# Moving the rotation of the queries from VectorE to GpSimd, with the halves placed by DMA

## The reference

```python
# 1: linear attention, 32 heads of 8
qkv = relu(x @ Wqkv.T);  vk = [v, 1]^T k per head;  y = (vk q)[:8] / (vk q)[8];  y @ Wp.T + bp
# 2: cross attention, 16 heads of 16, keys and values from ctx
q = rope2d((x @ Wq.T).astype(float16), pos);  k = rope2d((ctx @ Wk.T).astype(float16), pos)
softmax(q k^T / 4) v @ Wo.T + bo
# 3: low-rank FFN
gelu(x @ U1 @ V1 + b1) @ U2 @ V2 + b2
```

## Time and profile before

| | |
|---|---|
| Time, median of 3 runs (lowest to highest) | 702.24 us (699.44 to 704.75) |
| The profiled execution | 699.2 us, of which the span is 697.4 us |
| Busy in the span | TensorE 566.8 us (81%), VectorE 460.2 (66%), ScalarE 344.3 (49%), GpSimd 283.2 (41%) |
| Mean granted TensorE clock | 0.905 of full speed |
| The chain that ended last, by engine | TensorE 55%, VectorE 20%, issue 12%, GpSimd 4%, ScalarE 4%, SP's queue 3%, DMA 2% |

### The profile page before, as it was taken

The page is one execution under the profiler, slowest core; times in us unless marked ns, Lnnn a source line. Parts: engine busy times, 40 slices in busy tenths (PEclk is TensorE's granted clock), DMA queues, the critical chain, the costliest instruction groups (busy, mean ns, idle before and its releaser), DMA issues.

```text
span 697.4 us, 11782 instructions
## 1 busy us (share of the span) xinstructions
PE 566.8 (81%) x4224; PEld 384.8 (55%) x4224; DVE 460.2 (66%) x954; ACT 344.3 (49%) x503; POOL 283.2 (41%) x305
## 2 busy tenths in 40 slices
PE   2664778979797979798888979797978677899994
PEld 1554555747474747475656656565655444455552
DVE  5226578787878777787878787878777852234344
ACT  5220235646364646364545455554645545655551
POOL 4454304336353536262626262626161422232344
PEclk9987889999898989898989898989897978999998
DMA  7632101010202010101010101111000000113232
GB/s 273 143 99 59 40 0 55 2 53 3 67 4 66 6 64 7 62 9 62 12 58 24 45 24 47 31 39 48 7 24 1 24 16 16 46 49 117 90 120 91
DMA packets 24650, 34.94 MB, mean 50 GB/s; under 512 B 5080, under 2 KB 10840, under 8 KB 24600
## 3 DMA queue, kind: packets, MB, share of 16 engines
q1 hardware_dynamic: 23880, 33.85, 15.2%
q10 hardware_dynamic: 720, 0.43, 0.2%
HBM read 23.51 MB, written 8.65 MB: 46 GB/s over the span
## 4 chain that ended last, share of the span: by engine, by line
PE 55%; DVE 20%; issue 12%; POOL 4%; ACT 4%; SPq 3%; DMA 2%; POOLq 0%; DVEq 0%; ACTq 0%
PE FR L1039 19%; PE BK L1205 8%; PE BK L1039 6%; PE SC L1163 5%; DVE q_grp L849 5%; PE FR L1121 5%; DVE nmax L900 4%; PE SC L1190 4%; DVE q_grp L848 4%; PE FR L1097 2%; PE FR L1250 2%; DVE lin_tm L812 2%; POOL rs L546 2%; POOL c_fm L551 2%; PE BK L1222 1%
## 5 line engine op out<-in xcount | busy, mean ns | idle before, releaser
L658 ACT ACTIVATE probs<-SC 128x1024 f32<-128x1024 f32 x128 | 130.7, 1021 | 91.1 <-PE SC L1190 91.0
L900 DVE TENSOR_REDUCE nmax<-SC 128x4 f32<-128x1024 f32 x128 | 156.1, 1220 | 26.9 <-PE SC L1163 25.8
L1205 PE MATMUL BK<-probs,v_aug 128*32 128x256 f32 x1024 | 81.6, 443 | 0.6 <-ACT probs L658 0.6
L482 POOL TENSOR_TENSOR rs<-ve,minus_half 128x2 f32<-128x2 f32 x16 | 11.2, 701 | 164.0 <-DVE nm L942 164.0
L1163 PE MATMUL SC<-k_blk,q_grp 48*128 48x512 f16 x256 | 54.4, 422 | 15.7 <-DVE nmax L900 15.4
L1121 PE MATMUL FR<-ident,lin_tm 128*128 128x128 f32 x64 | 16.8, 414 | 61.3 <-DVE lin_tm L812 61.3
L1190 PE MATMUL SC<-q_grp,k_blk 64*128 64x256 f16 x512 | 54.0, 292 | 3.7 <-ACT q_grp L616 1.8
L463 POOL TENSOR_TENSOR att_fm_l<-att_raw,att_fm_h 128x512 fp32r<-128x512 f32 x16 | 20.5, 1278 | 80.4 <-ACT att_raw L634 80.4
L728 ACT ACTIVATE probs<-SC,b_ff 128x512 f32<-128x512 f32 x64 | 39.8, 686 | 22.4 <-PE SC L1356 21.7
L1039 PE MATMUL FR<-w_qkv_h,xs_fm_h 128*128 128x512 f32 x64 | 29.8, 466 | 23.0 <-POOL xs_fm_l L427 13.8
L1205 PEld LDWEIGHTS BK<-probs,v_aug 128*32 128x32 f32 x1024 | 29.2, 121 | 33.0 <-issue 23.6
(11 more groups left out here) (170 smaller groups left out, 1660.7 us busy)
## 6 DMA issues: line engine op xcount, KB each, us to landing
x_fm<-in_x_fm SPq DMA_DIRECT2D x16, 256.0 KB, 3.0
c_fm<-in_c_fm SPq DMA_DIRECT2D x16, 256.0 KB, 3.6
x_tm<-in_x_tm SPq DMA_DIRECT2D x16, 256.0 KB, 2.7
x_kept<-x2b SPq DMA_DIRECT2D x16, 256.0 KB, 2.2
x_tm<-x_kept SPq DMA_DIRECT2D x16, 256.0 KB, 2.7
out<-c_fm SPq DMA_DIRECT2D x16, 256.0 KB, 2.0
k_blk<-k_rope SPq DMA_DIRECT2D x128, 16.0 KB, 1.8
cos_t<-rope_tables SPq DMA_DIRECT2D x1, 896.0 KB
```

Source lines behind the costliest of these rows:

```text
L658: act.activation(probs[:, j % 4], SB[:], ACT.Exp, scale=SCALE).then_inc(s_exp, 1)
L900: dve.tensor_reduce(nmax[:, t, :, 2 * q:2 * q + 2], SA[:].rearrange("p (s f) t -> p s f t", s=2), AX.X, ALU.max, negate=True).then_inc(s_m ...
L1205: mm = pe.matmul(BK[q // 2][HP * k:HP * (k + 1), (q % 2) * T:(q % 2 + 1) * T], v_aug[b % NB][:, t, HC * q + k], probs[:, j % 4, k], start= ...
```

## The change

- **Queries on GpSimd.** VectorE keeps only the swap of halves. GpSimd's new `rope_q` makes the products in `k_cos` and `k_sin` (shared with the keys) and their sum, over all 128 partitions, in a new tile `q_rope`. It stands behind `rope_k` in GpSimd's step, ahead of `keep_x2`.
- **Placing.** SP's new `place_q` moves the four blocks of 32 partitions of `q_rope` into `q_grp`, behind `place_k`. `scores1` waits for these transfers.
- **First norm.** `stats1` also writes minus the mean (`nm1`), and GpSimd multiplies it by the power it has just made; `norm1_shift` goes.
- **Filling.** The keys of batch 0 are rotated and placed in step -2 and not in -3; those of batch 1 are made, rotated and placed in step -1. In the filling steps `residual_bias` stands ahead of the rotations.
- **Store of x2.** `keep` no longer waits for its own store; two semaphores alternate, and the waits stand where the buffer is used again.

```diff
 def key_batch(b):
-    return b + 3 if b < -1 else b + 2 if b >= 0 else -1
+    return b + 2 if b >= 0 else {FIRST: 0, -1: 1}.get(b, -1)
 ...
+def place_q(n):                                   # SP
+    sp.wait_ge(s_q_rope, n + 1)
+    wait(sp, s_s2_mm, NQ * (n - 2))
+    grp = q_grp[n % NB][:].rearrange("p (c e) t -> p e c t", e=2)
+    for e in range(2):
+        for s in range(2):
+            src, dst = PR * (e + 2 * s), TR * s
+            sp.dma_start(grp[dst:dst + PR, e], q_rope[src:src + PR]).then_inc(s_q_placed[n % NB], 16)
 ...
 def keep(q):
     sp.wait_ge(s_x2b, q + 1)
-    sp.dma_start(a["x2"][q], x2b[:, q % 2]).then_inc(s_x2_out, 16)
-    sp.wait_ge(s_x2_out, 16 * (q + 1))
+    sp.dma_start(a["x2"][q], x2b[:, q % 2]).then_inc(s_x2_out[q % 2], 16)
 ...
-    if on(key_batch(b)):                          # SP's step
+    if b == -2:
+        place_k(0)
+    if b >= -1 and on(key_batch(b)):
         place_k(key_batch(b))
+    if on(b + 2):
+        place_q(b + 2)
 ...
+def rope_q(n):                                    # GpSimd
+    cos, sin = (t[:, n * T:(n + 1) * T].unsqueeze(1).broadcast_to([P, CC, T]) for t in (cos_t, sin_t))
+    pool.wait_ge(s_q2_ev, n + 1)
+    pool.wait_ge(s_k_rope, n + 1)
+    pool.tensor_tensor(k_cos[:], q16[:], cos, ALU.mult).then_inc(s_q_part, 1)
+    pool.wait_ge(s_q_rot, n + 1)
+    pool.tensor_tensor(k_sin[:], rot[:], sin, ALU.mult).then_inc(s_q_part, 1)
+    if n >= 1:
+        pool.wait_ge(s_q_placed[(n - 1) % NB], 16 * N_Q_DMA * ((n - 1) // NB + 1))
+    pool.wait_ge(s_q_part, 2 * n + 2)
+    pool.tensor_tensor(q_rope[:], k_cos[:], k_sin[:], ALU.add).then_inc(s_q_rope, 1)
 ...
-    pool.wait_ge(s_ve1, n + 1)                    # rstd1
+    pool.wait_ge(s_ve1, 2 * n + 2)
     pool.tensor_tensor(rs1[:], ve1[:], minus_half[:], ALU.pow).then_inc(s_rs1, 1)
+    pool.wait_ge(s_rs1, n + 1)
+    pool.tensor_tensor(mr1[:], nm1[:], rs1[:], ALU.mult).then_inc(s_mr1, 1)
 ...
+    if b < 0:                                     # GpSimd's step
+        residual_bias(m)
+    if b == -2:
+        rope_k(0)
+    if b >= -1 and on(key_batch(b)):
         rope_k(key_batch(b))
+    if on(n):
+        rope_q(n)
     if on(q):
         keep_x2(q)
     if on(n):
         residual2(n)
-    if on(m):
+    if b >= 0 and on(m):
         residual_bias(m)
 ...
     turn_halves(rot, q16, s_q_rot)                # VectorE, rope_q
-    dve.tensor_tensor(q_cos[:], q16[:], cos, ALU.mult).then_inc(s_q_part, 1)
-    dve.wait_ge(s_q_rot, n + 1)
-    dve.tensor_tensor(q_sin[:], rot[:], sin, ALU.mult).then_inc(s_q_part, 1)
-def rope_q_sum(n):
 ...
-    for s in range(2):
-        src, dst = TR * s + PR, TR * s
-        dve.tensor_tensor(grp[dst:dst + PR, 0], q_cos[dst:dst + PR], q_sin[dst:dst + PR], ALU.add)
-        ins = dve.tensor_tensor(grp[dst:dst + PR, 1], q_cos[src:src + PR], q_sin[src:src + PR], ALU.add)
 ...
+    dve.tensor_scalar(nm1[:], mv1[:, :, 0], -1.0, None, ALU.mult).then_inc(s_ve1, 1)    # stats1
-def norm1_shift(n):
 ...
-    wait(pe, s_v2_ev, m if m < 3 else m - 1)      # q1
+    wait(pe, s_v2_ev, m if m < 2 else m - 1)
 ...
-    pe.wait_ge(s_q_rope, n + 1)                   # scores1, first chunk
+    pe.wait_ge(s_q_placed[n % NB], 16 * N_Q_DMA * (n // NB + 1))
```

More of the change, by code:

```diff
@@ L143, in build @@
         mr1 = sb("mr1", [P, TT])
+        nm1 = sb("nm1", [P, TT])
         nm2 = sb("nm2", [P, TT])
@@ L151, in build @@
         rot, k_rot = sb("rot", [P, CC, T], F16), sb("k_rot", [P, CC, T], F16)
-        q_cos, k_cos = sb("q_cos", [P, CC, T], F16), sb("k_cos", [P, CC, T], F16)
-        q_sin, k_sin = sb("q_sin", [P, CC, T], F16), sb("k_sin", [P, CC, T], F16)
+        k_cos = sb("k_cos", [P, CC, T], F16)
+        k_sin = sb("k_sin", [P, CC, T], F16)
         k_rope = sb("k_rope", [P, CC, T], F16)
+        q_rope = sb("q_rope", [P, CC, T], F16)
         q_grp = [sb(f"q_grp{i}", [P, HC, T], F16) for i in range(NB)]
@@ L211, in build @@
         s_k_const = sem("s_k_const")
-        s_x2_out = sem("s_x2_out")
+        s_q_placed = [sem(f"s_q_placed{i}") for i in range(NB)]
+        s_x2_out = [sem(f"s_x2_out{i}") for i in range(2)]
         s_x2_in = [sem(f"s_x2_in{i}") for i in range(2)]
@@ L263, in build @@
         N_W_REST = 8
-        N_K_DMA = 8
+        N_K_DMA, N_Q_DMA = 8, 4
         FIRST = -3
@@ L407, in _ @@
             for h in range(2):
+                sp.wait_ge(s_x2_out[h], 16)
                 fetch(0, h)
@@ L410, in _ @@
             keep(LAST)
+            for h in range(2):
+                sp.wait_ge(s_x2_out[h], 16 * (B // 2))
             with sp.Fori(0, NFB - 1) as i:
@@ L450, in rope_k @@
                 pool.wait_ge(s_k2_ev, n + 1)
+                wait(pool, s_q_rope, n)
                 pool.tensor_tensor(k_cos[:], k16[:], cos, ALU.mult).then_inc(s_k_part, 1)
@@ L491, in keep_x2 @@
                 pool.wait_ge(s_x2, 2 * q + 2)
-                wait(pool, s_x2_out, 16 * (q - 1))
+                wait(pool, s_x2_out[q % 2], 16 * (q // 2))
                 pool.tensor_tensor(x2b[:, q % 2], x2_tm[:],
@@ L505, in step @@
                     att_lo(p)
-                if on(key_batch(b)):
+                if b < 0:
[3 more added lines that the diff above has]
+                if b >= -1 and on(key_batch(b)):
                     rope_k(key_batch(b))
+                if on(n):
+                    rope_q(n)
                 if on(q):
@@ L830, in rope_q @@
                 turn_halves(rot, q16, s_q_rot)
[L831 to L836, removed]
-                dve.tensor_tensor(q_cos[:], q16[:], cos, ALU.mult).then_inc(s_q_part, 1)
-                dve.wait_ge(s_q_rot, n + 1)
-                dve.tensor_tensor(q_sin[:], rot[:], sin, ALU.mult).then_inc(s_q_part, 1)
-            def rope_q_sum(n):
-                wait(dve, s_s2_mm, NQ * (n - 2))
-                dve.wait_ge(s_q_part, 2 * n + 2)
-                grp = q_grp[n % NB][:].rearrange("p (c e) t -> p e c t", e=2)
-                for s in range(2):
-                    src, dst = TR * s + PR, TR * s
-                    dve.tensor_tensor(grp[dst:dst + PR, 0], q_cos[dst:dst + PR], q_sin[dst:dst + PR], ALU.add)
-                    ins = dve.tensor_tensor(grp[dst:dst + PR, 1], q_cos[src:src + PR], q_sin[src:src + PR], ALU.add)
-                ins.then_inc(s_q_rope, 1)
             def lint(n):
@@ L877, in stats1 @@
                 dve.tensor_scalar(ve1[:], mv1[:, :, 1], LN_EPS, None, ALU.add).then_inc(s_ve1, 1)
-            def norm1_shift(n):
-                dve.wait_ge(s_rs1, n + 1)
-                dve.scalar_tensor_tensor(mr1[:], mv1[:, :, 0], -1.0, rs1[:], ALU.mult, ALU.mult).then_inc(s_mr1, 1)
+                dve.tensor_scalar(nm1[:], mv1[:, :, 0], -1.0, None, ALU.mult).then_inc(s_ve1, 1)
             def ev_x1(n):
@@ L962, in step @@
                     row_max(n1, 2)
-                if on(n):
-                    norm1_shift(n)
                 if on(p):
@@ L987, in step @@
                     add2(p)
-                if on(n):
-                    rope_q_sum(n)
                 if on(m):
@@ L1156, in scores1 @@
                     pe.wait_ge(s_k_const, 16 * 2 * NB)
+                    pe.wait_ge(s_q_zeros, NB)
                 if c == 0:
                     pe.wait_ge(s_k_placed[n % NB], 16 * N_K_DMA * (n // NB + 1))
-                    pe.wait_ge(s_q_rope, n + 1)
+                    pe.wait_ge(s_q_placed[n % NB], 16 * N_Q_DMA * (n // NB + 1))
                 wait(pe, s_max, NQ * n + c)
```

## The result

| | before | after |
|---|---|---|
| Median of the runs compared (4 each) | 703.5 us | 627.12 us (624.73 to 628.47) |
| The profiled execution, its span | 699.2, 697.4 us | 624.73, 622.9 us |
| Ratio after / before | | 0.8919, 95% interval 0.887 to 0.8969 |
| Mean granted TensorE clock | 0.905 | 0.963 |

What follows compares the result with a forecast made beforehand. VectorE's four sums ahead of the divide, with the TensorE clock lost behind them, were taken as the bound. Ten steps save 55.6 us, steps 1, 2 and 13 9.6, filling and step 0 7.8: 73.0 off 699.2, 626 us, range 610 to 656.

Steps and rivals of the forecast that it cites:

- The wait and the clock: Ahead of the divide: removing VectorE's four sums saves 3.95 us, TensorE's clock staying full 2.7, less 0.6; 28.0 us a step.
- The placing path as the limit: Step's end: queries through GpSimd, SP and DMA land just after TensorE arrives, setting the step at 28.5 us.
- Work counted as nothing: Norm's product on GpSimd, 0 to 0.70 us, and keep's dropped wait on SP: both counted as no change in time.
- Steps 1 and 2: Two early steps, 32.06 and 33.54 us before, also to take 28.5: 3.6 and 5.0 us saved.
- Step 13: A step without divide, 25.81 us before: 1.0 us saved, bounds 2 lost and 3 saved.
- The filling: Before step 0: first scores at 64.2 to 64.8 instead of 67.5, 3.0 us saved; step -1 saves 2.4 us.
- The clock's loss: Rival, chance 0.12: gaps at the step's end keep TensorE's clock low, a step of 30.7 us, 652 us in all.
- the late placing: Rival, chance 0.14: dearer issues or slow landing of the queries add 2 to 4 us a step, 650 to 674 us.
- GpSimd stretches VectorE's work: Rival, chance 0.04: GpSimd and VectorE hinder each other, rope_q takes twice its 3.6 us, 644 us in all.

Runs made afterwards that it cites:

- Experiment 5: The changed kernel with GpSimd's rotation of the keys ahead of the low part of the attention output from step 0 on; 616.43 us.
- experiment 3: The changed kernel with twelve spare statistics instructions on VectorE ahead of the divide in steps 0 to 12, about 4.0 us; 694.65 us.
- experiment 2: The changed kernel with six spare statistics instructions on VectorE ahead of the divide in steps 0 to 12, about 2.0 us; 649.87 us.
- experiment 9: The changed kernel with the norm's product back on VectorE and SP again waiting for the store of x2; 624.8 us.
- experiment 4: The changed kernel with four more transfers per batch into a spare tile, between the four that place the queries; 682.48 us.
- Experiment 10: The changed kernel with keys rotated first and x of batch 2 loaded early (604.8 us), plus add2 moved behind row maximum 6 on VectorE; 607.84 us.
- experiment 8: The changed kernel with the queries' two products and one full-width sum back on VectorE, the placing by four transfers kept; 633.56 us.

## Why the prediction was right, step by step

The forecast was 626 us. The sum was made against the profiled execution, and that came out at 624.73; the median came out at 627.12.

- **The wait and the clock.** Put at 3.95 + 2.7 us less 0.6 for row maximum 6, a floor of 28.0 us a step. Experiment 5 has it bare at 28.0; experiment 3 shows wait and clock coming back together. Of the 2.7 us that the clock cost, the projection's part was taken too large: its twelve products take 1.61 us at full clock, not the 1.42 of the output projection with which they were compared, so 0.82 us and not 1.01 came back there. The clock's part was the least certain, argued from one step of the earlier trace rows; at the 2.1 us of gap of experiment 2 it fell in five of eleven steps.
- **The placing path as the limit.** Put at 28.5, measured 28.58, and right as a mechanism for eight of the ten steps. The other two were set by the shift and `add1` on VectorE, a path that the prediction did not have; that they came out at nearly the same length is luck. The parts: issues of the queries 2.6, measured 2.50; landing 1.8 from the issue, 1.9 at the median; from the last issue's end to the scores 1.2 to 1.8, measured 1.36; GpSimd's three 3.6, measured 3.6 (302.14 to 305.72 in the timeline). place_k's 8 issues were taken at 5.65 and took 5.98.
- **Work counted as nothing.** The norm's product and keep's wait: experiment 9 confirms it. The product itself took 0.20 us on GpSimd, against bounds of 0 and 0.70.
- **Steps 1 and 2.** 3.6 and 5.0 predicted, 4.0 and 5.9 measured. They came out at 28.07 and 27.65 us, below the 28.5 that I took over from the later steps. Step 2 ends by the third path; beyond that it was not followed why.
- **Step 13.** 1.0 gained was predicted, 0.9 lost: the step starts and ends with the clock low in part, and the path through eight and four issues is bare, 3.6 us of waiting. It lay within the bounds given (2 lost).
- **Step 14** was left out of the sum and gained 2.3 us: the same work stands there, but the clock is back sooner, as in the turns of L1235, 0.79 and 0.44 us in the chain against 1.04 and 0.85 before. Steps 13 and 14 together came out at 1.4 gained, against 1.0 summed.
- **The filling.** 5.4 up to step 0, measured 6.2. The load that lands late was put at 47.9 and came at 48.4; the first scores at 64.2 to 64.8, came at 64.26.
- **The rivals.** The clock's loss and the late placing did not happen here, but both are real further on: experiments 2 and 4. That GpSimd stretches VectorE's work happened, though not as the rival had it: GpSimd's own rotation kept its 3.6 us, but the shift's second operation takes 808 ns on average after, against 181 before. In most steps the wait for the placing hides it; at the end of step 2 and of the first two like steps it stands on the chain.

```profile
L926 DVE TENSOR_SCALAR shift<-nmax_c 128x32 f16<-128x32 f32 x16 | 12.9, 808 | 0.6
```

In experiment 10 such operations stood on the path in the step shown. The Trainium skill (GPSIMD Engine Reference, Key points) names VectorE's instructions in a 2-port mode beside those with two SBUF inputs. This one reads a single SBUF tensor; that it slows down fits the page, while no run here shows its mode. The Trainium skill's advice to keep elementwise work on VectorE (GPSIMD Engine Reference, Engine selection) is borne out only where nothing disturbs VectorE, 0.42 us against GpSimd's 1.15 for a half-precision operation of 128x512: experiment 8 followed it, and there the second product and the sum took 1.37 and 1.38 us on VectorE in nine of ten steps, longer than on GpSimd.

## What to carry to other kernels

Cost an edit by the gap that it closes on the engine that sets the step, and count the clock with it: here 4 us of idle TensorE cost another 2.7 us. When work moves off that path, compute the next path's end as carefully as the saving; here the sum of the placing's issues came within 0.1 us of the mean step. Look also at what stays on the engine that was relieved: operations of 0.18 us that were off the path took up to 1.2 us beside the other engine's work and, in some steps, came onto it. If an operation is split into pieces only to move data between partitions, one full-width operation and a few small transfers can be the shorter way, provided that the transfers have several us before they are needed; that it beats moving the pieces to another place in the order was not tried here.

## What was not expected of the hardware

The clock is not a function of the gap alone: with one and the same gap of 2.1 us it fell in five of eleven steps and not in the others (experiment 2), which spread otherwise like steps from 29.6 to 32.7 us. And the small shift operations on VectorE, 128 partitions of 32 elements, went from about 0.18 us to 1.17 us in one step when GpSimd worked beside them:

```profile
310.24 1.17 DVE L926 TENSOR_SCALAR shift<-nmax_c 128x32 f16<-128x32 f32 x1
```
